# Layer 1 scatters both expert choices quarter by quarter into two buffers, and merges the two when a group is loaded

## The chip, the core and the metric

One core of a Trainium2 chip runs the whole program in one launch. Its engines have each their own instruction stream and meet only at semaphores: TensorE (PE, matmuls and transposes), VectorE (DVE), ScalarE (ACT), GpSimd (POOL, which also issues the indirect DMAs) and SyncE (SP, which issues the plain DMAs). The metric is the time of one execution in microseconds on the device; the median of several runs counts.

## The reference

Two layers over x of shape (128, 32, 128), which is T = 4096 tokens of H = 128 features, all in float32. Layer 0 (a matmul per subject, and a top-1 mixture of 16 experts with a shared expert) is not touched by the change. Layer 1 is, cut to what matters:

```
x = layernorm(x + adapter(x, language)) * gamma + beta
gates = softmax(x @ router_w)                       # 4096 tokens, 8 experts
idx1  = argmax(gates);  mask1 = one_hot(idx1)
idx2  = argmax(gates * (1 - mask1));  mask2 = one_hot(idx2)
pos1  = cumsum(mask1) - mask1                       # place in the expert's list
pos2  = cumsum(mask2) - mask2 + sum(mask1)          # second choices come behind all first ones
mask1 = mask1 * (pos1 < 1280);  mask2 = mask2 * (pos2 < 1280)
g1, g2 = gate weights of the kept choices, divided by their sum
out   = g1 * expert[idx1](x) + g2 * expert[idx2](x) + 0.1 * shared_expert(x) + x
```

An expert is w2 @ silu(w1 x + b1) + b2 with 512 hidden features. Each of the 8 experts has a capacity of 1280 rows, so 10240 rows in all. A second choice can be placed only when all first choices of its expert have been counted, over all 4096 tokens.

## The kernel before

Tokens lie in 32 tiles of 128 (NT = 32); four tiles are one step (G = 4, NG = 8 steps), eight tiles a quarter (RT = 8).

**Layer-1 loop (lines 987 to 1028 on DVE, 1349 to 1408 on PE, 691 to 716 on ACT).** It is a software pipeline over the 8 steps. Step n transposes and multiplies by the adapter's first weights, step n - 1 by the second ones (L1381), then comes the layer norm on DVE (L1001 to L1007, then L1013 and L1015) and ACT, step n - 3 computes the router's logits (L1403) and copies them to `lg` (L1025). After every second step a quarter of the tokens has its logits: DVE finds each token's first choice (`first_max`, L795 to L799, and a running count, L952), PE turns counts into places (`rank1`, L1329 to L1332), and DVE turns places into row numbers (`first_slots` and `choice_slots`, L938 to L946). PE waits at `rank1` for DVE.

**Behind the loop.** DVE computes the softmax (L1039 to L1048), and then, over all 32 tiles at once, the second choices (L1052 to L1063). PE meanwhile computes the shared expert of layer 1: for each of 8 steps an up part (L1342 to L1344), whose input DVE splits into a high and a low part (`split_features`, L981 and L982), and a down part (L1417), whose result DVE adds to `acc` (`add1`, L1034 and L1036).

**Scatter.** POOL writes each token's row (128 features and one code that tells where the result belongs) to `rows1` in HBM with one indirect DMA for each tile and choice, 64 in all (L568). The first 32 follow the quarters, the other 32 wait until the second choices have their row numbers. First and second choices of a token differ in the code only; between the halves POOL rewrites the code column (L575). `rows1` was filled with zeros at the program's beginning (SP, L393), since not every row is used.

**Expert groups.** SP waits for all 64 scatters, and then loads `rows1` in 40 groups of 256 rows into five buffers `grp_x` (L451), in order, five groups for each expert. For group q, PE transposes it (`q_tr`, L1145 by its helper), multiplies by w1 in three passes (`q_up`, L1447 to L1449) and by w2 (`q_down`, L1459). ACT copies the transposed rows (L596) and applies silu (L735). DVE computes the low part of the input (`q_low`, L1089), the row numbers of the result (`q_index`, L1084) and adds b2 (`q_result`, L1102). POOL scatters the result to `back1` (L586). The order on PE in stage q is: wait for the low part of q, transpose q + 1, up q, down q - 1. The order on DVE in stage q is: index q + 2, low part q + 2, result q, and in two of ten stages the split of the next expert's weights (L1094, L1096). The last stage loads `back1` and adds both choices, weighted, to `acc` (L1134, L1139).

Of the kernel before, what the change touches and what calls it, by code (L numbers as in the profile page):

```python
# [5 lines left out]
def adaln_moe_two_layers(  # L6
# [29 lines left out]
    fp32 = mybir.dt.float32  # L36
    bf16 = mybir.dt.bfloat16
# [27 lines left out]
    TINY = 1.1920929e-07  # L65

# [28 lines left out]
    rows1 = nc.dram_tensor("rows1", (E1 * CAP, ROW), fp32).ap()  # L95
    back1 = nc.dram_tensor("back1", (TOP_K * T, H), fp32).ap()
# [6 lines left out]
    rows1_q = rows1.rearrange("(q u p) r -> q p u r", p=P, u=U)  # L103

    ctx = ExitStack()
    with ctx:
# [29 lines left out]
        grp_x = [sb(f"grp_x{k}", [P, U, ROW]) for k in range(NX)]  # L136
        grp_y = [sb(f"grp_y{k}", [P, U, H]) for k in range(2)]
# [6 lines left out]
        used = (2 * NG + 4 + 2) * GP + 10 * F1 + 2 * NX * ROW + 4 * H + 4 * GP + 2 * NCH * P  # L144
# [63 lines left out]
        before = sb("before", [P, E1], bf16)  # L208
        keep = sb("keep", [P, W])
        rst = sb("rst", [P, W])  # L210
        rst1 = sb("rst1", [P, E1 * RT])
# [108 lines left out]
        codes1 = sem("codes1")  # L320
        sc1 = [[sem(f"sc1_{k}{h}") for h in range(2)] for k in range(2)]
# [44 lines left out]
        def _(sp):  # L366
# [25 lines left out]
            for r in range(0, E1 * CAP, P * 4):  # L392
                sp.dma_start(rows1[r:r + P * 4, :].rearrange("(p a) r -> p (a r)", p=P),  # L393
                             zrow[:, 0:zw]).then_inc(zero1, 16)
# [61 lines left out]
            for k in range(TOP_K):  # L456
                for h in range(2):
                    sp.wait_ge(sc1[k][h], 16 * (NT // 2))
# [28 lines left out]
        def _(pool):  # L487
# [22 lines left out]
                    allow_small_or_imprecise_dtypes=True).then_inc(poolk, 1)  # L510
            gp.iota(jrow[:, :], pattern=[[P, NBLKP]], base=0, channel_multiplier=0,
# [7 lines left out]
            pool.wait_ge(poolk, 19)  # L519
# [39 lines left out]
            pool.wait_ge(zero1, 16 * (E1 * CAP // (4 * P) + TOP_K * T // (8 * P)))  # L559
            HT = NT // 2  # L560
            for k in range(TOP_K):
                for t in range(NT):
                    if k == 0 and t % RT == 0:
                        pool.wait_ge(slots1, t // RT + 1)
                        pool.wait_ge(b_tk, (t + RT) // G)
                    if k == 1 and t == 0:
                        pool.wait_ge(slots1, NT // RT + 1)
                    gp.indirect_dma_start(rows1, bass.IndirectOffsetOnAxis(ap=slot[:, k, t:t + 1], axis=0),  # L568
                                          disp[:, t, :], None, bounds_check=E1 * CAP - 1,
                                          oob_is_err=False).then_inc(sc1[k][t // HT], 16)  # L570
                    if (k, t) in ((0, NT - 8), (1, HT - 8)):
                        h = k
                        pool.wait_ge(sc1[0][h], 16 * HT)
                        half = slice(h * HT, (h + 1) * HT)
                        gp.tensor_scalar(disp[:, half, H:ROW], codes[:, half].unsqueeze(2), float(-T), None,  # L575
                                         ALU.add).then_inc(codes1, 1)
                        pool.wait_ge(codes1, h + 1)
# [14 lines left out]
        def _(eng):  # L592
# [125 lines left out]
            eng.wait_ge(ex_in, 1)  # L718
            sc.activation(t1[:, 0:NT * E1], t1[:, 0:NT * E1], ACT.Exp).then_inc(ex_out, 1)
            eng.preload_act_table(ACT.Silu)  # L720
            for n in range(1, NG):
                shared1_silu(n)

# [38 lines left out]
        def _(dve):  # L762
# [17 lines left out]
            dve.wait_ge(poolk, 19)  # L780
# [153 lines left out]
            def choice_slots(k, i0, n, pos):  # L934

                cols = slice(k * WE + i0 * E1, k * WE + (i0 + n) * E1)

                link(v.scalar_tensor_tensor(out=keep[:, cols], in0=pos, scalar=float(CAP), in1=mask[:, cols],  # L938
                                            op0=ALU.is_lt, op1=ALU.mult))
                link(v.tensor_tensor(et(t3[:, cols], n), et(pos, n), bc(baseE[:, :].unsqueeze(2), [P, E1, n]),  # L940
                                     ALU.add))
                if k == 0:
                    v.engine_nop().then_inc(b_rk, 1)
                link(v.tensor_tensor(t3[:, cols], t3[:, cols], keep[:, cols], ALU.mult))
                link(v.tensor_reduce(slotF[:, k, i0:i0 + n], by_t(t3[:, cols], n), AX.X, ALU.add))
                v.tensor_scalar(slot[:, k, i0:i0 + n], slotF[:, k, i0:i0 + n], float(DROP), None,  # L946
                                ALU.add).then_inc(slots1, 1)

            def first_choices(r):
                cols = slice(r * RT * E1, (r + 1) * RT * E1)  # L950
                first_max(lg, E1, t2, by_t(mask[:, cols], RT), r * RT, RT)
                link(v.tensor_tensor_scan(seen[:, cols], rst1[:, :], mask[:, cols], 0.0, ALU.mult, ALU.add))  # L952
                v.engine_nop().then_inc(mk1, 1)

            def first_slots(r):
                dve.wait_ge(pe_rank1, r + 1)
                last = et(seen[:, r * RT * E1:(r + 1) * RT * E1], RT)[:, :, RT - 1]
                if r == 0:
                    link(v.tensor_copy(before[:, :], last))
                else:  # L960
                    link(v.tensor_tensor(before[:, :], before[:, :], last, ALU.add))
                choice_slots(0, r * RT, RT, PS[7][:, WE:WE + RT * E1])
# [24 lines left out]
            for n in range(NG + 3):  # L987
# [4 lines left out]
                if (n - 3) * G % RT == 0 and n > 3:  # L992
                    first_slots((n - 3) * G // RT - 1)
# [28 lines left out]
                if n >= 3:  # L1022
# [3 lines left out]
                    if (m + 1) * G % RT == 0:  # L1026
                        dve.wait_ge(b_lc, m + 1)
                        first_choices((m + 1) * G // RT - 1)
# [13 lines left out]
            first_slots(NT // RT - 1)  # L1042
            split_features(1)
            split_features(2)
# [5 lines left out]
            parts = lambda a: a.rearrange("p (r e i) -> p r i e", e=E1, i=RT)  # L1050
            rie = lambda a: a.rearrange("p (r i e) -> p r i e", e=E1, i=RT)
            link(v.tensor_scalar(rie(t2[:, 0:WE]), parts(mask[:, 0:WE]), -1.0, 1.0, ALU.mult, ALU.add))  # L1052
            link(v.tensor_tensor(t2[:, 0:WE], lg[:, 0:WE], t2[:, 0:WE], ALU.mult))
            first_max(t2, E1, t1, by_t(mask[:, WE:2 * WE], NT), 0, NT)
            link(v.tensor_tensor_scan(seen[:, WE:2 * WE], rst[:, 0:WE], mask[:, WE:2 * WE], 0.0, ALU.mult, ALU.add))
            v.engine_nop().then_inc(mk1, 1)
# [485 lines left out]
```

## Time and profile before

| | us |
|---|---|
| median of 3 runs | 534.56 (533.38 to 535.95) |
| the profiled execution, its own time | 532.79 |
| its span, first to last instruction | 531.0 |
| PE busy | 447.7 (84%) |
| POOL busy | 256.3 (48%) |
| ACT busy | 247.4 (47%) |
| DVE busy | 240.2 (45%) |
| chain that ended last: PE | 63% |
| the same: POOL, and issue time | 12% each |

Busy time tells how much an engine has to do over the whole span; which engine sets the end is told by the chain of waits, and it changes from stage to stage. The mean granted clock of TensorE was 0.939 of full speed.

### The profile page before, as it was taken

The numbers are of one execution on the slowest core, as the hardware profiler recorded it, in microseconds if no ns is written. First come the engines' busy times: TensorE is split into PE (matmuls) and PEld (weight loads), VectorE is DVE, ScalarE is ACT, GpSimd is POOL, SyncE is SP. The second block draws the span as 40 slices with busy tenths as digits, with TensorE's granted clock in tenths as the row PEclk, the third lists the DMA queues.
The fourth block names the chain that finished last, engine by engine and source line by source line (L and its number), as shares of the span: only waits on it lengthen the run. The fifth ranks groups of instructions, "written<-read, shape, count | busy, mean of one in ns | idle before, by whom it ended". The sixth has DMA issues, their size and how long they took to land.

```text
span 531.0 us, 9984 instructions
## 1 busy us (share of the span) xinstructions
PE 447.7 (84%) x3129; PEld 384.3 (72%) x3130; DVE 240.2 (45%) x708; ACT 247.4 (47%) x593; POOL 256.3 (48%) x272
## 2 busy tenths in 40 slices
PE   6798879965999998899997879918999999999900
PEld 4698746644777775477786869908999999999800
DVE  1344486422555554244868865212333233323237
ACT  2234486202555553356456534403555555555424
POOL 3003567771555555500246777760555555655510
PEclk8989999996999999899999799977999999999965
DMA  9999921111322220800001111113234324331169
GB/s 255 398 308 356 393 63 45 55 50 46 78 71 68 78 64 8 237 10 2 11 30 42 45 51 46 55 40 100 66 116 123 107 68 141 109 79 34 35 175 307
DMA packets 66131, 57.96 MB, mean 109 GB/s; under 512 B 9485, under 2 KB 53152, under 8 KB 66099
## 3 DMA queue, kind: packets, MB, share of 16 engines
q1 hardware_dynamic: 58402, 43.99, 27.7%
q0 software_dynamic: 7168, 12.51, 7.3%
q10 hardware_dynamic: 528, 1.05, 0.5%
q8 instruction: 18, 0.29, 0.2%
q14 instruction: 15, 0.11, 0.1%
HBM read 30.28 MB, written 29.47 MB: 113 GB/s over the span
## 4 chain that ended last, share of the span: by engine, by line
PE 63%; POOL 12%; issue 12%; DVE 5%; DMA 5%; ACT 1%; POOLq 1%; SPq 0%; DVEq 0%; ACTq 0%
PE PS L1459 13%; PE PS L1145 8%; POOL rows L568 7%; PE PS L1189 6%; PE PS L1381 4%; POOL rows L536 4%; PE PS L1268 4%; PE PS L1447 4%; PE PS L1448 4%; PE PS L1449 4%; PE PS L1253 2%; PE PS L1255 2%; PE PS L1254 2%; PE PS L1368 2%; PE PS L1206 2%
## 5 line engine op out<-in xcount | busy, mean ns | idle before, releaser
L586 POOL DMA_INDIRECT back<-grp_y,grp_i x80 | 79.6, 996 | 71.9 <-DVE grp_y L1102 58.0
L568 POOL DMA_INDIRECT rows<-disp,slot x64 | 64.9, 1014 | 66.8 <-DVE slot L946 47.2
L1459 PE MATMUL PS<-w2r,act 128*128 128x128 f32 x640 | 77.7, 275 | 0.0
L1459 PEld LDWEIGHTS PS<-w2r,act 128*128 128x128 f32 x640 | 74.7, 191 | 0.0
L735 ACT ACTIVATE act<-PS,b1r 128x256 f32<-128x256 f32 x160 | 62.8, 475 | 14.5 <-PE PS L1449 14.5
L547 POOL DMA_INDIRECT back<-act,blk_i x48 | 47.0, 980 | 42.0 <-DVE act L906 21.3
L1102 DVE TENSOR_TENSOR grp_y<-PS,b2r 128x256 f32<-128x256 f32 x40 | 17.0, 425 | 89.3 <-PE PS L1459 84.4
L596 ACT ACTIVATE xh<-PS 128x256 fp32r<-128x256 f32 (+1 forms) x48 | 20.0, 418 | 74.2 <-PE PS L1145 74.2
L1447 PE MATMUL PS<-xh,w1h 128*128 128x256 f32 x160 | 48.3, 302 | 0.0
L526 POOL TENSOR_TENSOR w_gul<-w_raw,w_guh 128x512 fp32r<-128x512 f32 x16 | 21.0, 1336 | 50.1 <-ACT w_guh L596 50.1
L1448 PE MATMUL PS<-xl,w1h 128*128 128x256 f32 x160 | 44.9, 281 | 0.0
L1449 PE MATMUL PS<-xh,w1l 128*128 128x256 f32 x160 | 44.9, 281 | 0.0
L1189 PE MATMUL PS<-c0w,xT 128*32 x256 | 32.6, 291 | 7.3 <-issue 7.3
L536 POOL DMA_INDIRECT rows<-disp,slot x32 | 31.7, 990 | 13.0 <-issue 8.5
L1189 PEld LDWEIGHTS PS<-c0w,xT 128*32 128x32 f32 x256 | 29.4, 118 | 10.1 <-issue 9.0
L1417 PE MATMUL PS<-sw,act 128*128 128x128 f32 x256 | 33.6, 295 | 3.0 <-DVE acc L1036 3.0
L1417 PEld LDWEIGHTS PS<-sw,act 128*128 128x128 f32 x256 | 33.3, 212 | 3.8 <-issue 3.4
L687 ACT ACTIVATE act<-PS,sb 128x512 f32<-128x512 f32 x32 | 21.6, 688 | 26.2 <-PE PS L1344 26.1
L1268 PEld LDWEIGHTS PS<-w_dn,act 128*128 128x128 f32 x192 | 25.5, 190 | 9.7 <-issue 9.2
L1268 PE MATMUL PS<-w_dn,act 128*128 x192 | 30.1, 279 | 1.1 <-ACT act L596 1.1
L1449 PEld LDWEIGHTS PS<-xh,w1l 128*128 128x128 f32 x160 | 30.2, 189 | 0.0
L1447 PEld LDWEIGHTS PS<-xh,w1h 128*128 128x128 f32 x160 | 30.2, 189 | 0.0
(216 smaller groups left out, 946.0 us busy)
## 6 DMA issues: line engine op xcount, KB each, us to landing
rows<-zrow SPq DMA_DIRECT2D x32, 258.0 KB, 5.4
grp_x<-rows SPq DMA_DIRECT2D x40, 129.0 KB, 2.3
w_raw<-in_f_gate_up SPq DMA_DIRECT2D x8, 512.0 KB, 7.7
back<-zrow SPq DMA_DIRECT2D x8, 512.0 KB, 6.9
back<-back SPq DMA_DIRECT2D x16, 256.0 KB, 4.6
blk_x<-rows SPq DMA_DIRECT2D x48, 64.5 KB, 1.8
acc<-in_x SPq DMA_DIRECT2D x8, 256.0 KB, 5.2
y0g<-back SPq DMA_DIRECT2D x8, 256.0 KB, 3.2
```

What stands on the lines that cost most here:

```text
L536: gp.indirect_dma_start(rows0, bass.IndirectOffsetOnAxis(ap=slot[:, 0, t:t + 1], axis=0), disp[:, t, :], None, bounds_check=NBLKP * P - 1, ...
L547: gp.indirect_dma_start(back0, bass.IndirectOffsetOnAxis(ap=blk_i[c][:, 0:1], axis=0), blk_y[s][:, :], None, bounds_check=last_token, oob_ ...
L568: gp.indirect_dma_start(rows1, bass.IndirectOffsetOnAxis(ap=slot[:, k, t:t + 1], axis=0), disp[:, t, :], None, bounds_check=E1 * CAP - 1, ...
L586: gp.indirect_dma_start(back1, bass.IndirectOffsetOnAxis(ap=grp_i[v % NX][:, u:u + 1], axis=0), grp_y[k][:, u, :], None, bounds_check=last ...
L735: sc.activation(act[k][:, c, 0:UP], PS[1 + k * (C1 // 2) + c // 2][:, (c % 2) * UP:(c % 2 + 1) * UP], ACT.Silu, bias=b1r[e][:, c:c + 1]).t ...
L1189: last = mm(PS[1 + b][0:S, i * H:(i + 1) * H], xT[n % 2][:, t * S:(t + 1) * S], c0w[:, ds(offs[t], H)], start=True, stop=True)
L1268: last = mm(PS[4 if k == 0 else 7][:, 0:H], blk_aT[k][:, c * P:(c + 1) * P], w_dn[:, ds(off + c * H, H)], start=c == 0, stop=c == C0 - 1)
L1417: last = mm(tile(PS[4], i), tile(act[n % 2][:, c, :], i), sw2[:, c, :], start=c == 0, stop=c == C1 - 1)
L1447: mm(y, high, xh[k][:, 0:UP], start=True, stop=False)
L1448: mm(y, high, xl[k][:, 0:UP], start=False, stop=False)
L1449: last = mm(y, low, xh[k][:, 0:UP], start=False, stop=True)
L1459: last = mm(PS[5 + k][:, u * P:(u + 1) * P], act[k][:, c, u * P:(u + 1) * P], w2r[e][:, c, :], start=c == 0, stop=c == C1 - 1)
```

## The change

The functions on DVE are `choices` and `quarter_slots`, which take the place of `first_choices`, `first_slots` and `choice_slots`; `first_max` stays as it is. Between `quarter_slots` and the three calls of `add1` and `split_features` behind the loop stand the softmax's first instructions, the mask `second` and the codes `codeQ`; behind them stand the rest of the softmax, the `keep` of second choices and the weights. Second choices are found together with the first ones, for each quarter, from the logits instead of from the softmax. They are scattered to a buffer of their own, `rows1b`, from the top of each expert's capacity down, since their final place is not known until all first choices are counted. A group is then loaded from both buffers, and DVE adds the second buffer's rows to the first one's, multiplied by a mask (`second`) that is 1 for row numbers at or above the expert's count of first choices.

```diff
+    rows1b = nc.dram_tensor("rows1b", (E1 * CAP, ROW), fp32).ap()
 # SP: zeros for both buffers (20 DMAs more), and a second load for each group
-            for r in range(0, E1 * CAP, P * 4):
+            for rows in (rows1, rows1b):
+                for r in range(0, E1 * CAP, P * 4):
...
                 sp.dma_start(grp_x[k][:, :, :], at(rows1_q, m)).then_inc(gx_ld[k], 16)
+                sp.dma_start(grp_z[k][:, :, :], at(rows1b_q, m)).then_inc(gx_ld[k], 16)
 # POOL: 16 scatters for each quarter, no rewriting of the codes
+            for r in range(NR):
+                pool.wait_ge(slots1, r + 1)
+                pool.wait_ge(b_tk, (r + 1) * RT // G)
+                for k, rows in ((0, rows1), (1, rows1b)):
+                    for t in range(r * RT, (r + 1) * RT):
+                        gp.indirect_dma_start(rows, bass.IndirectOffsetOnAxis(ap=slot[:, k, t:t + 1], axis=0),
+                                              disp[:, t, :], None, bounds_check=E1 * CAP - 1,
+                                              oob_is_err=False).then_inc(sc1[k], 16)
 # DVE, in the loop, after every second step
+            def choices(r):
+                cols = quarter(r)
+                one, two = (chosen(mask, r, k).rearrange("p e i -> p i e") for k in range(TOP_K))
+                first_max(lg, E1, t2, one, r * RT, RT)
+                link(v.tensor_tensor(te(t1[:, cols], E1), te(lg[:, cols], E1),
+                                     bc(m1[:, r * RT:(r + 1) * RT].unsqueeze(2), [P, RT, E1]), ALU.subtract))
+                link(v.scalar_tensor_tensor(out=te(t2[:, cols], E1), in0=one, scalar=-BIG, in1=te(t1[:, cols], E1),
+                                            op0=ALU.mult, op1=ALU.add))
+                link(v.tensor_scalar(t2[:, cols], t2[:, cols], FLOOR, None, ALU.max))
+                first_max(t2, E1, t1, two, r * RT, RT)
+                both = slice(r * KQ, (r + 1) * KQ)
+                link(v.tensor_tensor_scan(seen[:, both], rst1[:, :], mask[:, both], 0.0, ALU.mult, ALU.add))
+                v.engine_nop().then_inc(mk1, 1)
+            def quarter_slots(r):
+                dve.wait_ge(pe_rank1, r + 1)
...
+                link(v.scalar_tensor_tensor(out=keep[:, both], in0=pos, scalar=float(CAP), in1=mask[:, both],
                                             op0=ALU.is_lt, op1=ALU.mult))
+                link(v.tensor_tensor(chosen(t3, r, 0), et(pos[:, 0:E1 * RT], RT),
+                                     bc(baseE[:, :].unsqueeze(2), [P, E1, RT]), ALU.add))
+                link(v.tensor_tensor(chosen(t3, r, 1), bc(baseE2[:, :].unsqueeze(2), [P, E1, RT]),
+                                     et(pos[:, E1 * RT:KQ], RT), ALU.subtract))
+                link(v.tensor_copy(lg[:, WE + r * E1 * RT:WE + (r + 1) * E1 * RT], pos[:, E1 * RT:KQ]))
+                v.engine_nop().then_inc(b_rk, 1)
+                link(v.tensor_tensor(t3[:, both], t3[:, both], keep[:, both], ALU.mult))
...
 # DVE, behind the loop
+            split_features(1)
+            link(v.tensor_scalar(sb2[:, :], sb2[:, :], SHARED_SCALE, None, ALU.mult))
+            quarter_slots(NR - 1)
+            add1(0)
+            split_features(2)
...
+            for n in range(1, 3):
+                add1(n)
+                split_features(n + 2)
...
+            split_features(5)
             for n in range(3, NG - 1):
                 add1(n)
                 if n + 3 < NG:
                     split_features(n + 3)
-            for n in range(3):
-                add1(n)
-                split_features(n + 3)
 # DVE, expert groups
+            def q_index(q, k):
+                dve.wait_ge(q_mg, q + 1)
+                v.scalar_tensor_tensor(out=grp_i[k][:, :], in0=grp_x[k][:, :, H], scalar=-1.0, in1=at_q(codeQ, q),
+                                       op0=ALU.mult, op1=ALU.add).then_inc(q_ix, 1)
+            def q_merge(q, k, turn):
+                dve.wait_ge(gx_ld[k], turn * 32 + 32)
+                for u in range(U):
+                    ins = v.scalar_tensor_tensor(out=grp_x[k][:, u, :], in0=grp_z[k][:, u, :],
+                                                 scalar=at_q(secondQ, q)[:, u:u + 1], in1=grp_x[k][:, u, :],
+                                                 op0=ALU.mult, op1=ALU.add)
+                ins.then_inc(q_mg, 1)
             def q_stage(q, b, it2=0, itg=0, it4=0, it16=0):
...
                 q_result(q, b % 2, b // GPE % 2, itg + b // 2 if b >= 2 else None)
+                if not (isinstance(q, int) and q + 3 >= NQ):
+                    q_merge(q + 3, (b + 3) % NX, it2 + (b + 3) // NX)
...
+            for q in range(3):
+                q_merge(q, q, 0)
             q_index(0, 0)
             q_low(0, 0)
 # PE, behind the loop and in the expert groups
-            rank1(NT // RT - 1)
             shared1_down(0)
+            rank1(NR - 1)
             shared1_up(1)
...
+            mm(PS[6][:, 0:E1], ones_b[:, :], before[:, 0:E1], start=True, stop=True).then_inc(pe_cnt1, 1)
+            for n in range(2, NG):
+                shared1_up(n)
+                shared1_down(n - 1)
-            def q_tr(k, turn):
-                pe.wait_ge(gx_ld[k], turn * 16 + 16)
+            def q_tr(q, k):
+                pe.wait_ge(q_mg, q + 1)
```

PE's stage q calls `q_tr(q + 1, k)`. On ACT the exponential of the softmax moves behind the shared expert's second step. POOL gets two small `iota` instructions more at the beginning.

## Rows read from the trace of the kernel before

**Rows 1.** Windows: us, busy us of PE, PEld, DVE, ACT, POOL (count), clock, DMA share, GB/s.
```profile
290.00:300.00 10.00, 7.58 (x45) 6.97 (x46) 7.05 (x22) 5.66 (x8) 7.39 (x7) 0.66 0.13 42
300.00:315.00 15.00, 11.11 (x74) 9.46 (x73) 11.10 (x24) 5.47 (x8) 11.08 (x13) 1.00 0.14 45
420.00:460.00 40.00, 40.00 (x352) 40.00 (x351) 12.49 (x39) 23.09 (x60) 23.21 (x24) 1.00 0.41 117
```

**Rows 2.** Timeline (start, us, engine, line, [idle before <- releaser]), PE and DVE in one group's stage.
```profile
402.10 0.38 PE L1145 MATMUL PS<-ident,grp_x 128*128 128x128 f32 x2
402.30 0.42 DVE L1102 TENSOR_TENSOR grp_y<-PS,b2r 128x256 f32<-128x256 f32 x1 [2.37 <-PE PS L1459]
402.64 0.16 DVE L1084 TENSOR_SCALAR grp_i<-grp_x 128x2 int32<-128x2 f32 x1
405.52 0.38 PE L1145 MATMUL PS<-ident,grp_x 128*128 128x128 f32 x2
```

**Rows 3.** Timeline, DVE in the last stage: four instructions of the merge's kind.
```profile
517.02 1.13 DVE L1134 SCALAR_TENSOR_TENSOR acc<-back,wk,acc 128x128 f32<-128x128 f32 x4
```

**Rows 4.** Timeline, PE released by DVE behind the loop.
```profile
310.45 0.69 DVE L1036 TENSOR_TENSOR acc<-acc,sb 128x512 f32<-128x512 f32 x1
311.29 0.68 PE L1417 MATMUL PS<-sw,act 128*128 128x128 f32 x4 [3.01 <-DVE acc L1036]
```

**Rows 5.** Timeline, POOL in the layer-1 scatter.
```profile
261.70 0.99 POOL L568 DMA_INDIRECT rows<-disp,slot  x1 [38.09 <-DVE slot L946]
278.28 0.98 POOL L568 DMA_INDIRECT rows<-disp,slot  x1 [6.61 <-DVE slot L946]
290.78 1.37 POOL L568 DMA_INDIRECT rows<-disp,slot  x1 [2.54 <-DVE slot L946]
355.02 0.98 POOL L568 DMA_INDIRECT rows<-disp,slot  x1 [0.30 <-issue]
```

**Rows 6.** Timeline, SP and PE around the first group.
```profile
342.92 3.74 PE L1417 MATMUL PS<-sw,act 128*128 128x128 f32 x32
357.37 3.55 SPq L451 DMA_DIRECT2D grp_x<-rows  x6
359.70 0.66 PE L1145 MATMUL PS<-ident,grp_x 128*128 128x128 f32 x2 [13.04 <-DMA grp_x<-rows]
360.15 5.70 PE L1417 MATMUL PS<-sw,act 128*128 128x128 f32 x32
```

**Rows 7.** Timeline, DVE between the logits of the first quarter and its slots.
```profile
255.92 0.22 DVE L795 TENSOR_REDUCE m<-lg 128x8 f32<-128x64 f32 x1
257.43 0.29 DVE L952 TENSOR_TENSOR_SCAN seen<-rst,mask 128x64 bf16<-128x64 f32 x1
259.37 0.17 DVE L959 COPY before<-seen 128x8 bf16<-128x8 bf16 x1 [0.69 <-PE PS L1330]
260.79 0.69 DVE L1001 TENSOR_TENSOR nrm<-PS,acc 128x512 f32<-128x512 f32 x1
```

**Rows 8.** Timeline, PE from the first rank matmul to the second choices' one.
```profile
259.17 1.58 PE L1381 MATMUL PS<-a_w,act 128*128 128x128 f32 x12
279.60 2.92 PE L1381 MATMUL PS<-a_w,act 128*128 128x128 f32 x24 [0.48 <-DVE mv L1007]
293.60 1.09 PE L1145 MATMUL PS<-ident,featT 128*128 128x128 f32 x4
306.47 0.17 PE L1427 MATMUL PS<-before,ones_b 128*128 128x8 bf16 x1 [0.88 <-DVEq L1056]
```

**Rows 9.** Timeline, the shared expert: PE's first up matmul in steps 3 and 4.
```profile
314.86 0.47 PE L1342 MATMUL PS<-xh,sw1h 128*128 128x512 f32 x1
321.19 0.48 PE L1342 MATMUL PS<-xh,sw1h 128*128 128x512 f32 x1
```

**Rows 10.** Timeline, SP's zeros and the scatter of layer 0 on POOL.
```profile
27.22 25.00 SPq L393 DMA_DIRECT2D rows<-zrow  x20
79.75 1.18 POOL L536 DMA_INDIRECT rows<-disp,slot  x1 [3.56 <-ACT disp L637]
```

More of the change, by code:

```diff
@@ L136, in adaln_moe_two_layers @@
         grp_x = [sb(f"grp_x{k}", [P, U, ROW]) for k in range(NX)]
+        grp_z = [sb(f"grp_z{k}", [P, U, ROW]) for k in range(NX)]
         grp_y = [sb(f"grp_y{k}", [P, U, H]) for k in range(2)]
@@ L319, in adaln_moe_two_layers @@
         codes0 = sem("codes0")
-        codes1 = sem("codes1")
-        sc1 = [[sem(f"sc1_{k}{h}") for h in range(2)] for k in range(2)]
+        sc1 = [sem(f"sc1_{k}") for k in range(TOP_K)]
+        cnt_ready = sem("cnt_ready")
+        pe_cnt1 = sem("pe_cnt1")
+        q_mg = sem("q_mg")
         s_sp = sem("s_sp")
@@ L456, in _ @@
             for k in range(TOP_K):
-                for h in range(2):
-                    sp.wait_ge(sc1[k][h], 16 * (NT // 2))
+                sp.wait_ge(sc1[k], 16 * NT)
             for m in range(NX):
@@ L555, in _ @@
                 residual(gp, pool, n)
[L559 to L577, printed above, removed]
+            pool.wait_ge(zero1, 16 * (TOP_K * E1 * CAP // (4 * P) + TOP_K * T // (8 * P)))
+            for r in range(NR):
[6 more added lines that the diff above has]
+                                              oob_is_err=False).then_inc(sc1[k], 16)
             last_row = pool.to_reg(TOP_K * T - 1)
@@ L949, in first_choices, with quarter @@
[L949 to L962, printed above, removed]
+            def quarter(r):
+                return slice(r * RT * E1, (r + 1) * RT * E1)
@@ L1118, in _ @@
             add1(NG - 1)
-            q_index(1, 0)
+            q_index(1, 1)
             q_low(1, 1)
@@ L1324, in rank1 @@
             def rank1(r):
-                cols = slice(r * RT * E1, (r + 1) * RT * E1)
-                pos = PS[7][:, WE:WE + RT * E1]
+                both = slice(r * KQ, (r + 1) * KQ)
+                pos = PS[7][:, WE:WE + KQ]
                 pe.wait_ge(mk1, r + 1)
                 pe.wait_ge(b_lc, (r + 1) * RT // G)
-                mm(pos, tri[:, :], mask[:, cols], start=True, stop=False)
-                last = mm(pos, ones_b[:, :], seen[:, cols], start=False, stop=r == 0)
+                mm(pos, tri[:, :], mask[:, both], start=True, stop=False)
+                last = mm(pos, ones_b[:, :], seen[:, both], start=False, stop=r == 0)
                 if r:
                     last = mm(pos.rearrange("p (e i) -> p e i", i=RT), ones_b[:, :],
-                              before[:, :].unsqueeze(2).to_broadcast([P, E1, RT]), start=False, stop=True)
+                              before[:, :].unsqueeze(2).to_broadcast([P, TOP_K * E1, RT]), start=False, stop=True)
                 last.then_inc(pe_rank1, 1)
@@ L1461, in q_down, with q_stage @@
                 last.then_inc(q_dn, 1)
-            def q_stage(q, w, e, we, k, turn, weights=None, first=False, last=False):
+            def q_stage(q, w, e, we, k, weights=None, first=False, last=False):
                 pe.wait_ge(q_xl, q + 1)
                 if not last:
-                    q_tr(k, turn)
+                    q_tr(q + 1, k)
                 if weights is not None:
```

119 lines of the change are left out of this document (63 added, 56 removed).

## The prediction

> **What bounds the kernel now.** I read the windows first, then the timeline of single stages, since the change touches three: the layer-1 loop, the shared expert with the scatter beside it, and the expert groups. In the groups PE is busy all of 40.00 us at full clock while DVE has 12.49 and POOL 23.21 us of work [rows 1]: a pause of PE is paid in full there, and DVE's mean load says nothing about when its work comes. One group takes PE 405.52 - 402.10 = 3.42 us [rows 2]. Ahead of it PE stands for 13.04 us until the first load lands [rows 6], and the clock has fallen meanwhile, as the next down part shows (5.70 us against 3.74 for the same 32 matmuls [rows 6]). That load waits for POOL: 64 scatters, the last issued at 355.02 [rows 5]. The change aims at this gap.
>
> **Term 1: the scatter ends earlier.** POOL starts at 261.70, and pauses before 278.28 and 290.78 for DVE's row numbers [rows 5]; from there 48 scatters run to 355.02, so one each (355.02 - 290.78) / 47 = 1.37 us, code rewriting included; I take 1.32 without it. With 16 scatters a quarter POOL has work of 21 us for each, more than the 16.6 and 12.5 us between the quarters, so that it no longer pauses. The start moves by what DVE does more in the first quarter (term 2: 2.5 us), to 264.2. The last is issued at 264.2 + 63 x 1.32 = 347.4, 7.6 us earlier, and the first group's transpose could start at 359.70 - 7.6 = 352.1; the second load is issued one slot later (3.55 / 6 = 0.6 us [rows 6]) and two merging instructions (0.57 us, below) follow: 353.3. Bounds for this: 1.28 to 1.37 us a scatter, 350.8 to 356.5.
>
> **Term 2: PE gets there later.** (a) DVE's choices of a quarter cost 257.43 + 0.29 - 255.92 = 1.80 us now, its slots 260.79 - 259.37 = 1.42 [rows 7]. The change adds a second `first_max` (1.51 us, the start of L795 to that of L952), three instructions of 64 elements (0.26 each as in those five; one reads the mask across, as L799 does in 0.45), and doubles the scan: 2.5 us. The slots get two instructions more (0.26 each) and double width on four: 0.85 us. In the first two quarters DVE has idle time, but PE meets it at the rank matmuls, which it issues between two halves of L1381, at 259.17 in the first quarter [rows 8]: DVE was done at 257.72 [rows 7], 1.45 us earlier, so that 2.5 us more cost PE 1.05 and a release of 0.15, 1.2 us. I take 1.8 for the second quarter, where DVE's lead is smaller. From 279.60 on PE waits for DVE (0.48 us there [rows 8]), and every addition counts: 0.85 (second quarter's slots), 2.5, 0.85. Sum at the end of the last transpose: 1.2 + 1.8 + 0.85 + 2.5 + 0.85 = 7.2 us, 294.7 [rows 8] becomes 301.9. Bounds: 4.2 (the last three alone) to 10.
> (b) Behind the loop PE's waits of 0.88 [rows 8] and 3.01 us [rows 4] for second choices go. The first down part follows a sparse stretch and runs at the low clock as now, 5.4 us (5.70 in the like case [rows 6]): 307.3. Up 1 takes 2.8 us. Up 2 needs `split_features(2)`, now behind the last slots (2.3 us), `add1(0)` (2 x 0.69 less their overlap, 1.35 [rows 4]) and its own 1.1 us: 312.4. An up and a down part are 321.19 - 314.86 = 6.3 us [rows 9], of which down is 3.5, so that down 1 ends at 318.7.
> (c) The splits stand one step later: before, `add1(n)` was followed by the split for n + 3, now by that for n + 2. So up 3 waits for `add1(1)` and split 3, which wait for down 1: 1.35 + 1.1 + 0.2 = 2.65 us, and up 4 in the same way. Up 3 starts at 321.4 instead of 314.86 [rows 9], and with the second wait PE reaches the first group's transpose 6.5 + 2.65 = 9.1 us later: 342.92 + 3.74 + 9.1 = 355.8. The weights' arithmetic ahead of split 5 (5 us) has 6.3 us of PE's work to hide in.
> So PE, not the scatter, is last: 355.8 against 353.3. That gains 359.70 - 355.8 = 3.9 us. PE no longer stands long before down 7, which takes 5.7 us at the low clock and 3.74 at the full one [rows 6]: 2.0 more. Together 5.9 us gained; between a loss of 2 and a gain of 11.
>
> **Term 3: the merge in each group.** What counts is its place. DVE's stage q is: index and low part of q + 2, result q, merge q + 3. The result of q waits for `q_down(q)`, which PE issues at the end of its stage q + 1. PE's stage q + 2 begins with the transpose of q + 3, which now waits for merge q + 3. So PE finishes a down part, and the very next thing it has queued waits until DVE has taken the result of that same down part and then merged. Nothing covers this: the up part, the next down part, ACT's copy and silu stand behind that transpose in PE's order. Before, the transpose waited for a load that had landed stages earlier. Price: the transpose would start at 402.10; DVE takes up the result at 402.30 and can start its next instruction at 402.64 [rows 2]; two merges of 128 x 129 elements at 1.13 / 4 = 0.28 us each [rows 3] end at 403.21; PE starts about 0.15 us after DVE's end (310.45 + 0.69 = 311.14, then 311.29 [rows 4]). 403.36 - 402.10 = 1.26 us. Register work for the masks' moving addresses can hide in the result's 0.42 us. The first three merges are done in advance, so the transposes of groups 3 to 39 pay: 37 x 1.26 = 46.6 us. Lower bound, one merge hidden and no release time: 0.85 x 37 = 31 us; upper, 0.3 us of register work on top: 1.56 x 37 = 58 us.
>
> **The rest, near nothing.** The first three merges wait for the third pair of loads (6 x 0.6 us after the first); `q_low(0)` behind them is due when down 7 ends, 4 us after the transpose. Loads double in bytes; the DMA share is 0.41 [rows 1], and a merge asks for them three stages after SP may issue them. `q_index` grows from one operation to two at the same size. The 20 more zero DMAs take SP and the DMA engines 25 us [rows 10], which SP has, since its next work waits for layer 0's scatter. They now run beside the first of these scatters, at 79.75 [rows 10]; there I allow 0 to 3 us, since a scatter took 1.37 instead of 0.98 us now and then [rows 5], and put 0.5 into the sum. Two `iota`s at the start: DVE is waiting for loads shortly after.
>
> **Sum.** On the profiled execution: 532.79 - 5.9 + 46.6 + 0.5 = 574.0. The median shown is 1.8 us above that execution: 575 to 576 on the scale of the median, and I take 575.
>
> **Rivals.**
> (1) *The merges are out of PE's way, the change pays.* If DVE had merged q + 3 before `q_down(q)` ends, term 3 would be zero and 534.56 - 5.9 = 529 us would come out, at best 524. It decides itself at the order of DVE's stream: only if the merge stood before `q_result` or PE's transpose a stage later. For it speaks DVE's idle time of 2.37 us right before the result [rows 2]; against it, that this idle time is the wait for `q_down` itself, and the merge stands behind that wait. 5 in 100.
> (2) *The pauses bring TensorE's clock down.* Each stage would be 3.42 us of work and 1.26 of nothing, busy 73%. Rows on both sides: 290 to 300 had PE busy 76% and a clock of 0.66, 300 to 315 had 74% and 1.00 [rows 1]. At the low level down 7 took 2.0 us more of 3.74 [rows 6], so that a stage would grow by 1.8 us: 37 x 1.8 = 67 us if it always ran so, 641 us; 597 if a third of the time. Behind the waits here come 3.4 us of dense matmuls, and in the 300 to 315 window such bursts held the full clock. 8 in 100, with 605 as its middle.
> The Trainium skill (TensorE: Matmul & The Clock Gate, A second HAM failure mode: psum-queue depth-cycling) speaks for this rival: brief idle times of PE between groups of matmuls made the clock go back and forth. By it the sum would be between 597 and 641; the two windows above agree with it once and contradict it once, and no row shows a pause of 1.3 us in every stage.
> (3) *The front doesn't gain.* If slots come so late that POOL pauses again, or PE's delays add up to 13 us, term 1 and 2 cancel, the clock falls as before, and term 3 is all: 534.6 + 47 = 582. 12 in 100.
>
> **Chances and range.** Forecast 75, rivals 5, 8 and 12. The forecast's own range, from the bounds of terms 2 and 3: 559 to 591. It holds rival 3 as well, and a little of rival 2; I give 560 to 593. Half a per cent (2.7 us) is about what a measurement of this kernel can tell from no change. Faster 0.05, the same 0.01, slower 0.94.
>
> **What would show it.** In the profile after: in the groups PE idle once a stage at the transpose (L1145 by its helper), released by DVE's merge, 37 times, 1.1 to 1.4 us each, and a stage of 4.7 us; DVE's order result, merge, merge without a pause between; POOL's 64 scatters without a long pause and the last issued near 347; waits of about 2.7 us before the up parts 3 and 4; the first group's transpose near 356, and no fall of the clock before it. The prediction is wrong if the transposes start without a wait, if the clock in the groups is below 1.00, or if layer 0 got longer by more than 3 us.

## The result, and the profile after

The changed kernel takes 585.33 us (median of 4 runs, 583.46 to 587.27), the kernel before 533.97 in the runs beside it (527.20 to 535.95): a ratio of 1.101 with an interval of 1.090 to 1.112. The prediction was 575 with a range of 560 to 593, slower; it holds. The profiled execution took 586.1 us, its span 584.2. The larger term, a wait in each expert group, came out almost as forecast (48.1 us for 46.6). The smaller one had the wrong sign: the front, which was to gain 5.9 us, lost 4.7, of which 1.6 lie ahead of layer 1.

Of the waits of PE in layer 1 of the changed kernel (engine, line waited for, us in total, times, longest), one line now outweighs all others; the next one is in the front:

```profile
PE PS L1188 <- DVE grp_x L1121: 43.9, 38, 3.2
PE PS L1385 <- DVE xl L1004: 7.5, 3, 2.8
```

L1188 is the transpose's helper, L1121 the merge, L1385 the first matmul of an up part and L1004 the split that it needs. One of the 38 is the first transpose (3.2 us), the other 37 are the groups 3 to 39. The timeline of one stage, DVE first, then PE (start, us, engine, line, in brackets the idle time before and what ended it), answers to [rows 2]:

```profile
385.56 0.42 DVE L1141 TENSOR_TENSOR grp_y<-PS,b2r 128x256 f32<-128x256 f32 x1 [2.32 <-PE PS L1497]
385.91 0.60 DVE L1121 SCALAR_TENSOR_TENSOR grp_x<-grp_z,second,grp_x 128x129 f32<-128x129 f32 x2
386.57 0.44 PE L1188 MATMUL PS<-ident,grp_x 128*128 128x128 f32 x2 [1.15 <-DVE grp_x L1121]
390.24 0.42 DVE L1141 TENSOR_TENSOR grp_y<-PS,b2r 128x256 f32<-128x256 f32 x1 [2.36 <-PE PS L1497]
391.25 0.44 PE L1188 MATMUL PS<-ident,grp_x 128*128 128x128 f32 x2 [1.04 <-DVE grp_x L1121]
```

The reader is to see the order: DVE waits for PE's down part (L1497), takes its result, merges twice without a pause, and PE starts 0.06 us after the merges' end (385.91 + 0.60 = 386.51, then 386.57). From transpose to transpose it is 4.68 us, where before it was 3.42. From the first transpose to the last:

```profile
L1188 PE MATMUL PS<-ident,grp_x x80: 272/273/332, 364.9 to 547.5; 128*128 128x128 f32 x80
```

182.6 us, and before 359.7 to 494.7, 135.0. The windows answer to [rows 1] (same columns):

```profile
325.00:329.00 4.00, 4.00 (x18) 3.31 (x17) 0.00 (x0) 2.40 (x4) 3.08 (x4) 0.66 0.17 55
336.00:340.00 4.00, 4.00 (x19) 3.38 (x18) 3.69 (x10) 2.75 (x4) 3.09 (x4) 0.75 0.15 50
366.00:368.00 2.00, 2.00 (x11) 2.00 (x11) 0.22 (x1) 0.00 (x0) 0.00 (x0) 0.50 0.29 73
420.00:460.00 40.00, 31.25 (x261) 29.73 (x260) 14.39 (x45) 17.38 (x45) 17.48 (x18) 1.00 0.43 121
```

In the groups PE is busy 78% and the clock stays at its full level. Behind the loop it does not: in the first three windows PE is busy without a gap at a mean clock of 0.66, 0.75 and 0.50 of full speed, each behind a wait of 2.6 to 3.2 us. Up part 2 took PE 317.20 - 314.30 = 2.90 us; parts 3 and 4, with the low clock, took 4.45 and 4.42. The rest of the timeline, PE, DVE and POOL in the front:

```profile
265.24 0.99 POOL L582 DMA_INDIRECT rows<-disp,slot  x1 [40.06 <-DVE slot L983]
346.95 0.97 POOL L582 DMA_INDIRECT rows1b<-disp,slot  x1 [0.30 <-issue]
261.54 0.23 PE L1372 MATMUL PS<-mask,tri 128*128 128x128 bf16 x1 [0.99 <-DVEq L960]
280.13 0.23 PE L1372 MATMUL PS<-mask,tri 128*128 128x128 bf16 x1 [1.44 <-DVEq L960]
295.91 0.23 PE L1372 MATMUL PS<-mask,tri 128*128 128x128 bf16 x1 [2.83 <-DVEq L960]
323.57 0.50 PE L1385 MATMUL PS<-xh,sw1h 128*128 128x512 f32 x1 [2.64 <-DVE xl L1004]
334.59 0.80 PE L1385 MATMUL PS<-xh,sw1h 128*128 128x512 f32 x1 [2.84 <-DVE xl L1004]
361.76 0.69 DVE L1056 SCALAR_TENSOR_TENSOR acc<-PS,acc 128x512 f32<-128x512 f32 x1 [4.90 <-PE PS L1460]
364.15 1.66 DVE L1121 SCALAR_TENSOR_TENSOR grp_x<-grp_z,second,grp_x 128x129 f32<-128x129 f32 x6
364.91 0.41 PE L1188 MATMUL PS<-ident,grp_x 128*128 128x128 f32 x2 [3.19 <-DVE grp_x L1121]
365.16 5.36 PE L1460 MATMUL PS<-sw,act 128*128 128x128 f32 x32
```

So the scatter did what it was meant to: it ends 8 us earlier (346.95 for 355.02 [rows 5]) and does not pause after its start. Where the 53.2 us of span went, by the same points of both traces:

| point | before | after | later by |
|---|---|---|---|
| first expert weights of layer 1 issued (layer 0 over) | 219.10 | 220.68 | 1.6 |
| up part 3 of the shared expert [rows 9] | 314.86 | 323.57 | 8.7 |
| first group's transpose [rows 6] | 359.70 | 364.91 | 5.2 |
| second group's transpose | 365.69 | 370.36 | 4.7 |
| last group's result | 503.23 | 556.04 | 52.8 |
| end of the span | 531.0 | 584.2 | 53.2 |

Between the second transpose and the last result the change loses 48.1 us.

### The profile page after: what moved, and what is told of

It is laid out like the page before. It is cut to its first block, busy times and chain, and to the rows that moved or that the text cites. A ratio compares the mean times of both kernels' runs of the same rounds, so it can differ in the third digit from the quotient of the medians.

```text
span 584.2 us, 10233 instructions
## 1 busy us (share of the span) xinstructions
PE 460.8 (79%) x3126; PEld 388.4 (66%) x3128; DVE 269.2 (46%) x818; ACT 247.4 (42%) x593; POOL 252.5 (43%) x272
## 4 chain that ended last, share of the span: by engine, by line
PE 65%; DVE 15%; issue 8%; POOL 5%; DMA 4%; ACT 1%; DVEq 1%; SPq 0%; POOLq 0%; ACTq 0%
PE PS L1497 12%; PE PS L1188 9%; PE PS L1232 6%; PE PS L1460 5%; POOL rows L553 4%; DVE grp_x L1121 4%; PE PS L1311 3%; PE PS L1486 3%; PE PS L1485 3%; PE PS L1424 3%; PE PS L1487 3%; PE PS L1296 2%; PE PS L1297 2%; PE PS L1298 2%; PE PS L1249 1%
## 5 line engine op out<-in xcount | busy, mean ns | idle before, releaser
L593 POOL DMA_INDIRECT back<-grp_y,grp_i x80 | 77.7, 971 | 134.7 <-DVE grp_y L1141 118.8
L1497 PE MATMUL PS<-w2r,act 128*128 128x128 f32 x640 | 77.7, 275 | 0.0
L1497 PEld LDWEIGHTS PS<-w2r,act 128*128 128x128 f32 x640 | 74.6, 191 | 0.0
L603 ACT ACTIVATE xh<-PS 128x256 fp32r<-128x256 f32 (+1 forms) x48 | 20.1, 418 | 112.4 <-PE PS L1188 112.4
L582 POOL DMA_INDIRECT rows<-disp,slot x32 | 31.8, 994 | 49.5 <-DVE slot L983 40.1
L1188 PE MATMUL PS<-ident,grp_x 128*128 128x128 f32 x80 | 17.2, 297 | 44.3 <-DVE grp_x L1121 43.9
L1188 PEld LDWEIGHTS PS<-ident,grp_x 128*128 128x128 f32 x80 | 8.1, 140 | 51.4 <-DVE grp_x L1121 38.5
L553 POOL DMA_INDIRECT rows<-disp,slot x32 | 31.5, 985 | 13.0 <-issue 8.5
L1232 PEld LDWEIGHTS PS<-c0w,xT 128*32 128x32 f32 x256 | 29.3, 118 | 10.8 <-issue 9.4
L582 POOL DMA_INDIRECT rows1b<-disp,slot x32 | 31.7, 990 | 9.7 <-issue 9.1
```

The lines of the kernel that those rows point to most:

```text
L553: gp.indirect_dma_start(rows0, bass.IndirectOffsetOnAxis(ap=slot[:, 0, t:t + 1], axis=0), disp[:, t, :], None, bounds_check=NBLKP * P - 1, ...
L582: gp.indirect_dma_start(rows, bass.IndirectOffsetOnAxis(ap=slot[:, k, t:t + 1], axis=0), disp[:, t, :], None, bounds_check=E1 * CAP - 1, o ...
L593: gp.indirect_dma_start(back1, bass.IndirectOffsetOnAxis(ap=grp_i[v % NX][:, u:u + 1], axis=0), grp_y[k][:, u, :], None, bounds_check=last ...
L1188: return nc.tensor.transpose(dst, src, ident[0:k, 0:k])
L1232: last = mm(PS[1 + b][0:S, i * H:(i + 1) * H], xT[n % 2][:, t * S:(t + 1) * S], c0w[:, ds(offs[t], H)], start=True, stop=True)
L1497: last = mm(PS[5 + k][:, u * P:(u + 1) * P], act[k][:, c, u * P:(u + 1) * P], w2r[e][:, c, :], start=c == 0, stop=c == C1 - 1)
```

## Experiments

The theory after the result had two parts: in the groups the place of the merge costs 48 us, and in front two orders in DVE's stream cost what the earlier scatter would have brought. The rivals were the doubled loads and DVE's extra work in themselves, and the zeros for the second buffer.

The experiments ran in four sets, each on another chip, with the kernel before in each. In one set it took 534 us, in the other three 592 to 598; traces from those three show pauses in the front that the traces of the first don't (last section). So times are compared only with the kernel before in the same set, and the groups by the trace from first to last transpose, which with the pauses came out 1.4 to 6.5 us longer.

**e1_merge_first and e1r_merge_first: the merge in front of the result.**

```diff
+                if not (isinstance(q, int) and q + 3 >= NQ):
+                    q_merge(q + 3, (b + 3) % NX, it2 + (b + 3) // NX)
                 q_result(q, b % 2, b // GPE % 2, itg + b // 2 if b >= 2 else None)
-                if not (isinstance(q, int) and q + 3 >= NQ):
-                    q_merge(q + 3, (b + 3) % NX, it2 + (b + 3) // NX)
```

> The changed kernel with DVE's merge of group q + 3 put in front of the result of group q instead of behind it; same loads, same merges, same masks. Theory (place of the merge): the 1.30 us a stage that the transposes wait go, 37 x 1.30 = 48 us off the profiled 586.1: 538, stages of 3.43 us, no PE wait at the transposes of groups 3 to 39. Rival (second load and DVE's extra work themselves): the loads and merges are all still there, so the time stays above 565. Whatever the front costs (5 us in the trace) stays.

Measured first in a set with the pauses: 615.8 us, before 591.86 (1.041, 1.031 to 1.050). In such a set neither the 538 us of the theory nor the rival's 565 can decide, since the kernel before is itself above both. The group stage is told by PE's transposes in its trace (the header is: minimum, median, maximum ns, first and last start):

```profile
L1188 PE MATMUL PS<-ident,grp_x x80: 272/273/331, 439.9 to 577.4; 128*128 128x128 f32 x80
its engine sat idle before it (us, times) until:
  DVE grp_x L1121: 3.2, 1
```

137.5 us instead of 182.6 (136.4 in e4's trace, which has the groups of the kernel before, in the same set), and of 38 waits only the first is left. All loads, merges and masks are still there.

> Merge in front of the result, as e1_merge_first, to have its time beside the next two. First to last transpose 137.5 us again, and the time 48 us below the changed kernel's: 538 where before takes 534. The front is that of the changed kernel: waits of 2.6 to 2.8 us ahead of the shared expert's up parts 3 and 4, and 3.2 us at the first transpose.

In a set without the pauses it took 535.95 us, before 534.49 (1.004, 1.000 to 1.008): 49 us less than the changed kernel's 585.33, where 48 were expected. From first to last transpose it took 134.0 us (370.4 to 504.4) and not 137.5 again; the kernel before has 135.0. Waits at up 3 and 4 were 2.64 and 2.83 us again, and 3.2 at the first transpose. The place of the merge is shown as the cause of the large term; the rival is out.

**e2_before_touch: only the wait and two instructions to wait for, on the kernel before.** PE's transpose and `q_index` wait for `q_mg`, as in the changed kernel, and DVE has, behind `q_result`:

```diff
+            def q_touch(k, turn):
+                dve.wait_ge(gx_ld[k], turn * 16 + 16)
+                for u in range(U):
+                    ins = v.scalar_tensor_tensor(out=grp_x[k][:, u, :], in0=grp_x[k][:, u, :], scalar=zrow[:, 0:1],
+                                                 in1=grp_x[k][:, u, :], op0=ALU.mult, op1=ALU.add)
+                ins.then_inc(q_mg, 1)
```

> The kernel before with nothing but a merge-like step: two scalar_tensor_tensor of 128 x 129 that add zero times the rows to themselves, behind the result as in the changed kernel, and PE's transpose waiting for them. No second load, no mask, no change in front. Theory: 37 stages x 1.30 us = 48 us more than before, 582, as PE waits right behind its own down part. Rival (the second load, DMA contention or the moving mask addresses are what costs): within 3 us of before, or at the most 0.6 us a stage, 556.

643.08 us where before took 591.86: 51 us, a ratio of 1.091 (1.078 to 1.104). PE's waits in its trace:

```profile
PE PS L1157 <- DVE grp_x L1091: 44.0, 38, 3.2
```

The same 38 waits with the same sum as in the changed kernel, without a second load and without a mask with a moving address; the longest, 3.2 us, is again the first transpose. From first to last transpose 183.0 us.

**e3b_merge_double: the price in instructions.** Behind the two merges stand two more of the same shape before PE is released:

```diff
+                for u in range(U):
+                    ins = v.scalar_tensor_tensor(out=grp_z[k][:, u, :], in0=grp_z[k][:, u, :],
+                                                 scalar=at_q(secondQ, q)[:, u:u + 1], in1=grp_z[k][:, u, :],
+                                                 op0=ALU.mult, op1=ALU.add)
                 ins.then_inc(q_mg, 1)
```

> The changed kernel with each merge followed by two more instructions of the same shape and kind, which overwrite the second buffer's tile after it has been used, before PE is released. Theory: the wait is made of the DVE instructions ahead of the release, so each stage grows by 2 x 0.27 = 0.54 us, and the first transpose to the last takes 182.6 + 37 x 0.54 = 203 us. Rival (the wait is mostly semaphore latency and restart of PE): 183 to 187 us.

```profile
L1192 PE MATMUL PS<-ident,grp_x x80: 272/286/448, 363.1 to 565.8; 128*128 128x128 f32 x80
```

202.7 us, 20.1 more than 182.6, or 0.54 a stage for two instructions. The time was 604.02 us (before 534.49). The wait grows by what DVE has to do ahead of the release, as the theory has it.

**e5_split_ahead: the front's first order.** On top of e1, the splits stand one step ahead again:

```diff
+            split_features(3)
             for n in range(1, 3):
                 add1(n)
-                split_features(n + 2)
+                split_features(n + 3)
...
-            split_features(5)
             for n in range(3, NG - 1):
```

> e1_merge_first, and the split of step n + 3 stands behind add1(n) again, as in the kernel before (split 3 is done ahead of add1(1), split 5 behind add1(2)). Theory (the lost lookahead costs the front): the two waits of 2.64 and 2.84 us ahead of up 3 and up 4 go, and with them the stretch at the low clock that follows them, 3 us: 8 us less than e1_merge_first. Rival (the rank waits of the loop and the early stages make the front late): at most 2 us less.

524.16 us, where e1 took 535.95 and before 534.49 in the same set: 11.8 us less than e1, and 0.979 (0.974 to 0.984) of before. PE's waits for the split; a window over the stretch of up 3 and up 4, and the first transpose with down 7 behind it:

```profile
PE PS L1385 <- DVE xl L1004: 2.0, 1, 2.0
```

```profile
322.00:326.00 4.00, 4.00 (x30) 3.70 (x29) 1.53 (x3) 0.87 (x2) 3.08 (x4) 1.00 0.16 50
353.47 0.41 PE L1188 MATMUL PS<-ident,grp_x 128*128 128x128 f32 x2 [3.19 <-DVE grp_x L1121]
353.71 3.74 PE L1460 MATMUL PS<-sw,act 128*128 128x128 f32 x32
```

5.5 us of waits are gone, and the clock, at 0.66 and 0.75 behind them in the changed kernel, is full. I had put 8 us on it; the medians differ by 12. The traces account for 10 of them: from the first expert weights of layer 1 (217.86 in e5, 220.68 in the changed kernel) to down 6 it is 128.7 us instead of 137.3, which is the 5.5 us of waits and 3.1 of low clock, and down 7 took 3.74 us instead of 5.36. The rest is not accounted for.

**e6_first_merge_early: the front's second order.** On top of e5, group 0 is merged ahead of `add1(6)`:

```diff
             for n in range(3, NG - 1):
+                if n == NG - 2:
+                    q_merge(0, 0, 0)
                 add1(n)
...
-            for q in range(3):
+            for q in range(1, 3):
                 q_merge(q, q, 0)
```

> e5_split_ahead, and the merge of group 0 stands ahead of add1(6) in DVE's stream instead of behind it and behind the split of the first weights. Theory: the 3.2 us that the first transpose waits go, and the down part behind it no longer runs at the low clock (5.4 us against 3.7): 3 to 5 us less than e5_split_ahead, which would put it below the kernel before by 4 to 8 us. Rival (the first loads have not landed then, so that PE waits for them all the same): no difference to e5_split_ahead.

523.29 us, 0.976 (0.971 to 0.981) of before. DVE and PE in its trace:

```profile
352.08 0.62 DVE L1115 SCALAR_TENSOR_TENSOR grp_x<-grp_z,second,grp_x 128x129 f32<-128x129 f32 x2 [3.92 <-DMA grp_z<-rows1b]
352.86 0.39 PE L1189 MATMUL PS<-ident,grp_x 128*128 128x128 f32 x2
354.62 3.81 PE L1461 MATMUL PS<-sw,act 128*128 128x128 f32 x32 [1.37 <-DVE acc L1058]
358.27 0.38 PE L1189 MATMUL PS<-ident,grp_x 128*128 128x128 f32 x2
```

The wait of 3.2 us at the first transpose is gone, 1.37 for the result of down 6 have come. From the start of down 6 to the second transpose it is 358.27 - 349.29 = 9.0 us, in e5 357.29 - 346.54 = 10.8: 1.8 us. The medians differ by 0.9 only, within their scatter, where 3 to 5 were expected. The clock part of what I expected here was moot: in e5 the down part 7 had already run at the full clock (3.74 us). Why it did is open: in the changed kernel too PE worked without a gap at the full clock for the 10 us ahead of its wait of 3.19 us, and there the clock fell behind it. What holds the first merge now is its own load (`[3.92 <-DMA grp_z<-rows1b]`, until 352.08).

> e5_split_ahead again with more rounds, to have an interval beside e6r: 524, 10 us below before.

> e6_first_merge_early again with more rounds. In its profile the 3.2 us wait at the first transpose is gone and 1.4 us of wait for the result of down 6 have come in, and the full clock holds: 3.5 us less than e5 from the end of down 6 to the second transpose. Theory: 2 to 4 us below e5r. Rival (given back later): no difference, as the medians of 524.16 and 523.29 have it.

These repeats fell into a set with the pauses: 606.53 and 603.94 us, before 598.33, ratios of 1.019 (1.009 to 1.030) and 1.020 (1.013 to 1.027). They don't settle e6 against e5, and they show that the gain over the kernel before is there only in the set without the pauses. They look like this in e6r's trace, between the four chunks of an up part:

```profile
376.11 0.69 ACT L694 ACTIVATE act<-PS,sb 128x512 f32<-128x512 f32 x1 [5.61 <-remote]
376.85 0.79 PE L1386 MATMUL PS<-xh,sw1h 128*128 128x512 f32 x1 [4.65 <-issue]
383.10 0.69 ACT L694 ACTIVATE act<-PS,sb 128x512 f32<-128x512 f32 x1 [6.30 <-remote]
383.84 0.80 PE L1386 MATMUL PS<-xh,sw1h 128*128 128x512 f32 x1 [5.35 <-issue]
```

**e8_front_only: e6 with the merges behind the result again.**

```diff
                 q_result(q, b % 2, b // GPE % 2, itg + b // 2 if b >= 2 else None)
+                if not (isinstance(q, int) and q + 3 >= NQ):
+                    q_merge(q + 3, (b + 3) % NX, it2 + (b + 3) // NX)
```

> The changed kernel with both repairs of the front (splits one step ahead, the merge of group 0 ahead of add1(6)), but with the merges of the groups behind the result as it has them. Theory (two separate costs that add up): the groups still take 182 us from first to last transpose, and the time is 585 less the 12 to 15 us of the front: 570 to 573. Rival (the group stage hides or eats the front's gain): above 580.

In the same set as e5r and e6r: 645.84 us, 42 more than e6r; from first to last transpose 607.1 - 424.3 = 182.8 us. The group term is there with either front. Whether the front's 12 us are gained in full beside it, 570 to 573 us in the expectation, can't be read off, since the changed kernel wasn't run in this set.

**e4_before_zeros and e4r_before_zeros: only the zeros.**

```diff
-            for r in range(0, E1 * CAP, P * 4):
+            for rows in (rows1, rows1b):
+                for r in range(0, E1 * CAP, P * 4):
```

> The kernel before with the 20 zero DMAs for a second row buffer and nothing else. In the changed kernel's trace layer 0's first block load is issued at 123.47 instead of 122.40 and the first expert weights of layer 1 at 220.68 instead of 219.10. Theory (the zeros slow the early stages): 1 to 2 us more than before in the profile at these two places. Rival (this is scatter between executions): both places within 0.4 us of before.

> The kernel before with the 20 zero DMAs more, as e4_before_zeros, again. In profiles so far the first expert weights of layer 1 are issued at 219.10 (before), 220.68 (changed), 217.86 (e5_split_ahead) and 220.63 us (e6_first_merge_early), the last three all with the zeros. Theory (the 1.6 us between the first two is scatter between executions): within 1 us of before in the median. Rival (the zeros cost layer 0 something): 1.5 to 3 us more than before.

595.0 us beside 591.86 (1.003, 0.998 to 1.009), and 593.95 beside 598.33. Both sets had the pauses, so a cost of 1 us can't be excluded by them. The better evidence are the traces without the pauses. All but one have the zeros, and they issue the first expert weights of layer 1 at 217.86 (e5), 218.00 (e3b), 220.63 (e6), 220.68 (the changed kernel) and 224.85 (e1r, an execution of 543.99 us); the kernel before, without them, at 219.10. So the 1.6 us of the table are within the scatter between executions, and a cost of the zeros is not shown; nor is one below that scatter excluded.

**e9_rank_later: the rank matmuls behind all four tiles.** On top of e6:

```diff
                     for i in range(G):
-                        if i == 2 and (n - 3) * G % RT == 0 and n > 3:
-                            rank1((n - 3) * G // RT - 1)
...
-                elif (n - 3) * G % RT == 0 and n > 3:
+                if (n - 3) * G % RT == 0 and n > 3:
                     rank1((n - 3) * G // RT - 1)
```

> e6_first_merge_early, and in the first two quarters PE issues the rank matmuls behind all four tiles of the adapter's second part instead of between two halves of it. Theory: PE's waits of 1.0 and 1.4 us at the rank matmuls (0.99 and 1.44 in the changed kernel's trace) shrink below 0.4 us each, since DVE has 1.4 us more, while DVE gets its ranks only 0.3 us later; 1 to 2 us less than e6_first_merge_early, a ratio to before of about 0.973. Rival (DVE is what bounds the last steps of the loop, so that PE's earlier arrival only waits there): the two waits go and the time does not move.

609.06 us beside 595.13 (1.025, 1.015 to 1.035), again in a set with the pauses and without e6 beside it; inconclusive for the time. In its trace the wait at the first quarter's rank matmul (0.99 us in the changed kernel) is gone, but that at the second one (1.44 there) is not:

```profile
290.31 0.22 PE L1373 MATMUL PS<-mask,tri 128*128 128x128 bf16 x1
321.10 0.29 PE L1373 MATMUL PS<-mask,tri 128*128 128x128 bf16 x1 [1.47 <-DVEq L960]
```

## Why the prediction was right, and where it was not

**Term 3, the merge in each group: right in mechanism and size.** 37 waits were forecast with 1.26 us each; measured are 48.1 / 37 = 1.30 us a stage, of which PE stands idle (43.9 - 3.2) / 37 = 1.10. Most of the rest is lost overlap: before, the transpose started 0.17 us ahead of the end of the down part (405.52 against 403.74 + 1.95 = 405.69). e1, e2 and e3b show the mechanism by removing it, by adding it alone, and by making it longer. The upper bound's register work for the moving address doesn't show in the trace: the first merge starts 0.35 us after the result's start, as the index did before (0.34 [rows 2]).

**Term 1, the scatter: right.** Start 265.24 (forecast 264.2), last issue 346.95 (347.4). The date that it was to give, 353.3 for the first transpose, is seen in e6, where the merge is not held up by DVE's other work: 352.86.

**Term 2 (a), the loop: right.** DVE's longer choices cost PE 0.99 and 1.44 us at the first two rank matmuls (forecast 1.2 and 1.8) and 2.83 at the third. The last transpose of the loop ends at 304.3; without the 1.6 us of scatter in layer 0 that is 302.7 for 301.9.

**Term 2 (c), the lost lookahead: right in mechanism, mis-sized.** The two waits were forecast with 2.65 us each and are 2.64 and 2.84. The term left out what follows a wait: up 3 and up 4 ran at a clock of 0.66 and 0.75. The waits are 5.5 us and the low clock another 3.1 (4.45 and 4.42 us for 2.90); e5 took 11.8 us less than e1r, of which the traces account for 10.

**The failed step: "PE, not the scatter, is last: 355.8".** PE was ready at 361.7 and the loads had been issued at 349.41, but the first transpose came at 364.91. I had the first merge wait for its load, and had not placed it in DVE's stream: it stands behind `add1(6)`, which waits for down 6, and behind the split of the weights (2.4 us from 361.76 to 364.15). That is what I asked of the groups, what is queued ahead of the merge on its engine, and had not asked at the first one. With it went the 2.0 us I had counted for down 7 at the full clock: it took 5.36 us. Measured against the forecast 355.8, the 9.1 us too many are 1.6 ahead of layer 1, 0.8 in the loop, 3.1 low clock in up 3 and 4, 3.2 this wait, and by subtraction 0.4 small change. e6 shows the wait's cause by moving the merge; by the trace it is worth 1.8 us and not 3.2, since down 7 needs `add1(6)`, which ends at 354.48, and waits 1.37 for it; the first wait used to cover that.

**The bounds.** The profiled execution took 586.1 us where 574.0 were forecast for it: of the 12.1 too many, 10.6 lie in the front (4.7 lost instead of 5.9 gained) and 1.5 in the groups. The front was given between a loss of 2 and a gain of 11, so it came out beyond its own bound (by 3.1 us of loss too, without what lies ahead of layer 1), while the groups came out well within theirs. That the sum is in the range all the same is owed to the width that term 3 and rival 3 gave it. (The bounds of terms 2 and 3 added up give about 555 to 595, not the 559 to 591 of the text.)

**Rival 1 (the merges out of PE's way)** did not happen, but is one moved line away: e1. Its price, 529 us, was too good by the front's loss (535.95). **Rival 2 (the clock in the groups)** did not happen: 1.00 in every window from 372 to 540 at a busy share of 75 to 78%. The Trainium skill (TensorE: Matmul & The Clock Gate, A second HAM failure mode: psum-queue depth-cycling) tells of another kernel, in bf16, where brief idle times between groups of matmuls made the clock go back and forth. That doesn't carry over to this stage, with 37 idle times of 1.10 us on average; here the measurement decides. The clock did fall in the front, behind waits of 2.6 to 3.2 us, though not behind every one: in e5 it stayed at 1.00 behind 3.19 us. **Rival 3 (the front doesn't gain)** happened in part: term 1 and 2 did not cancel at 0, they came to a loss of 4.7 us, 3.1 without what lies ahead of layer 1, with the low clock as this rival had it.

## What to carry to other kernels

When a consumer's wait moves from a DMA to an instruction on another engine, write down what stands ahead of that instruction in its engine's stream and what that in turn waits for; if it is the consumer's own last work, the two engines alternate and every stage pays. Do this for the prologue as well as for the loop. Here two moved lines in the loop and two orders in front turned 585 us into 523, 2.4% faster than the kernel before (0.971 to 0.981), in the set without the pauses; the second of the two orders has no gain in the median that is clear of scatter.

## What was not expected of the hardware

The same program ran at 534 us in two sets and at 592, 595 and 598 in three others, each of these on another chip. No chip was used twice, so that the chip and the time of running can't be told apart. In e4's trace, from one of the three, the first expert weights of layer 1 are issued at 244.15 instead of 219.10, so 25 us are added ahead of layer 1, and the first transpose comes at 420.9 instead of 359.7, so 36 more between these points; from first to last transpose it is 136.4 us instead of 135.0.

The pauses are not PE's alone. In the rows of e6r above (line numbers are those of its own kernel), PE waits for ACT to empty the same PSUM bank: its matmuls start at 376.85 and 383.84, 0.05 us after ACT's activations end (376.80 and 383.79), though the profile calls PE's wait "issue". ACT in turn stood 5.61 and 6.30 us before them, on what the profile calls "remote", another core or an unknown queue, while its input, up part 1, had been done since 358.8. In e6, without the pauses, four such activations take 2.76 us together. The longest wait of PE there, 17.13 us in e4r, is of the same kind, with DVE in ACT's place: DVE stood 25.69 us on "remote" ahead of `add1`, and PE started 0.15 us after its end. In e4 PE itself stops, by about 1.5 us, between matmuls of one chunk that wait for nothing in the program. The first two rows are e4r's, the last two e4's:

```profile
382.86 0.69 DVE L1038 TENSOR_TENSOR acc<-acc,sb 128x512 f32<-128x512 f32 x1
383.70 0.55 PE L1419 MATMUL PS<-sw,act 128*128 128x128 f32 x1 [17.13 <-issue]
380.92 0.59 PE L1345 MATMUL PS<-xl,sw1h 128*128 128x512 f32 x1 [1.52 <-issue]
383.00 0.59 PE L1346 MATMUL PS<-xh,sw1l 128*128 128x512 f32 x1 [1.50 <-issue]
```

In the sets with the pauses e6 is 2% slower than the kernel before instead of 2.4% faster. What causes the pauses, and why the reordered front meets more of them, stays open; it was not tried.
